# Last edge pass of a two-layer graph network kernel: projection in three passes, y one turn later, messages in PSUM, one-hot on ScalarE, another order of loads

## The reference

```python
# layer 0: attention over the edges of each receiver, 8 heads of 32
qkv = x @ W_qkv.T + b_qkv                      # Q, K, V
att = einsum('mhd,mhd->mh', Q[receivers], K[senders]) * INV_SQRT_DK
e = exp(att - seg_max[receivers]);  denom = segment_sum(e, receivers)[receivers]
out = segment_sum((e / denom)[:, :, None] * V[senders], receivers)
x = layernorm(x + out @ W_ff.T + b_ff)
# layer 1: messages from the senders' type embedding and the edge attributes
W = (edge_attr_64 @ W_dist + b_dist) * cut[:, None]
msgs = embed_table[node_type_100][senders] * W
agg = segment_sum(msgs, receivers)
x = layernorm(x + concatenate([x, agg], axis=1) @ W_comb + b_comb)
```

## Time and profile before

| | |
|---|---|
| median of 3 runs | 1124.53 us (1122.92 to 1125.94) |
| the profiled execution | 1127.21 us, span 1125.5 us |
| mean granted TensorE clock of the span | 0.978 |
| busy share: PE, DVE, ACT, POOL | 94%, 82%, 71%, 72% |
| span of the last edge pass | about 747 us to the end |

### The profile page before, as it was taken

The page is one execution under the profiler, slowest core; times in us unless marked ns, Lnnn a source line. Parts: engine busy times, 40 slices in busy tenths (PEclk is TensorE's granted clock), DMA queues, the critical chain, the costliest instruction groups (busy, mean ns, idle before and its releaser), DMA issues.

```text
span 1125.5 us, 25645 instructions
## 1 busy us (share of the span) xinstructions
PE 1058.2 (94%) x7302; PEld 983.2 (87%) x7302; DVE 918.4 (82%) x2643; ACT 802.3 (71%) x2452; POOL 811.4 (72%) x656
## 2 busy tenths in 40 slices
PE   5889999999999999999979799989999999999993
PEld 4679999999999999999858588879989888889882
DVE  5867888888888888888998889758888888888882
ACT  3876777777777777777767688875666666666663
POOL 5588878787888788886788888844666666666663
PEclk9999999999999999999989899989999999999997
DMA  4866666666666666665545457765666666666640
GB/s 152 305 241 215 229 228 229 224 231 221 228 217 230 208 232 216 231 219 207 190 166 200 158 206 238 276 195 164 177 174 186 188 183 186 186 189 193 186 140 33
DMA packets 121388, 227.26 MB, mean 202 GB/s; under 512 B 33588, under 2 KB 61487, under 8 KB 121185
## 3 DMA queue, kind: packets, MB, share of 16 engines
q1 hardware_dynamic: 104000, 189.54, 50.6%
q0 software_dynamic: 17248, 36.08, 11.3%
HBM read 137.84 MB, written 93.59 MB: 206 GB/s over the span
## 4 chain that ended last, share of the span: by engine, by line
PE 52%; DVE 26%; issue 10%; ACT 7%; SPq 2%; DVEq 1%; DMA 1%; POOL 0%; ACTq 0%; POOLq 0%
PE ps L852 7%; DVE num L1619 5%; PE ps L831 5%; PE ps L891 4%; PE ps L890 4%; PE ps L892 4%; PE ps L847 4%; PE ps L845 4%; PE ps L846 4%; DVE zeT L1630 3%; DVE est L1656 3%; DVE agg L1643 3%; PE ps L888 2%; ACT t L1196 2%; DVE msg L1639 2%
## 5 line engine op out<-in xcount | busy, mean ns | idle before, releaser
L682 POOL TENSOR_TENSOR zin<-xin,bff_row 128x1024 f32<-128x1024 f32 x98 | 233.1, 2379 | 39.3 <-DVE stat L1414 18.5
L1442 DVE SCALAR_TENSOR_TENSOR yn<-ps,r,bc 128x256 f32<-128x256 f32 x391 | 169.0, 473 | 64.0 <-PE ps L847 40.5
L852 PE MATMUL ps<-w_mix,zT 128*128 128x256 f32 x780 | 189.4, 394 | 10.1 <-ACT zT L1092 5.4
L852 PEld LDWEIGHTS ps<-w_mix,zT 128*128 128x128 f32 x780 | 147.8, 197 | 34.4 <-ACT zT L1092 10.7
L1107 ACT ACTIVATE junk<-yn 128x256 f32<-128x256 f32 x391 | 157.8, 415 | 12.3 <-DVE yn L1442 12.0
L743 POOL TENSOR_TENSOR ev<-abc,v 128x512 f32<-128x512 f32 x49 | 62.0, 1266 | 115.5 <-DVE zeT L1630 115.5
L1414 DVE BATCH_NORM_STATS2 stat<-zin 128x6 f32<-128x256 f32 x391 | 135.3, 407 | 1.9 <-issue 1.5
L724 POOL DMA_INDIRECT ty<-in_node_type_dram,src_i x98 | 103.2, 1053 | 25.7 <-issue 23.1
L730 POOL DMA_INDIRECT xd<-in_x_dram,idx x98 | 94.8, 967 | 36.1 <-PE ps L876 13.8
L755 POOL DMA_INDIRECT out_dram<-oe,idx x98 | 101.1, 1032 | 25.4 <-issue 20.2
L845 PE MATMUL ps<-mix_hi,z_hi 128*128 128x256 f32 x392 | 114.0, 291 | 2.8 <-DVE z_lo L1479 2.8
(11 more groups left out here) (212 smaller groups left out, 3377.0 us busy)
## 6 DMA issues: line engine op xcount, KB each, us to landing
xin<-in_x_dram SPq DMA_DIRECT2D x97, 512.0 KB, 4.4
out_dram<-on SPq DMA_DIRECT2D x97, 512.0 KB, 2.9
xd_o<-xdT SPq DMA_DIRECT2D x49, 256.0 KB
v_o<-vT SPq DMA_DIRECT2D x49, 256.0 KB, 2.0
v<-v_o SPq DMA_DIRECT2D x49, 256.0 KB
xd<-xd_o SPq DMA_DIRECT2D x49, 256.0 KB, 4.2
abc<-a_o SPq DMA_DIRECT2D x196, 64.0 KB
sbc<-same_o SPq DMA_DIRECT2D x49, 128.0 KB, 3.8
```

The source lines that it names most:

```text
L682: pool.tensor_tensor(z, xx, bb, ALU.add).then_inc(n_z, 1)
L852: last = mm(ps[0:np_, half(g, j), (j % 2) * D:(j % 2 + 1) * D], zT[:, g % 2, k, j * P:j * P + np_], w_mix[:, k, :], start=k == 0, stop=k = ...
L1442: last = dve.scalar_tensor_tensor(out=yn[0:np_, q, j * D:(j + 1) * D], in0=ps[0:np_, half(g, j), (j % 2) * D:(j % 2 + 1) * D], scalar=r1[0 ...
```

## The change

It edits the last edge pass alone, save for the weight's parts. (1) `ff` uses `wff_hi`, `wff_lo` and high and low parts of `num`, 12 fp32r matmuls in place of 4 fp32 ones; ScalarE makes the high part (`sum_high`), GpSimd the low part (`sum_low`), and VectorE once the low part of the weight. (2) VectorE's turn computes y of block i-3, not i-2, ahead of `edge_z`, so the second norm and the scatter come a turn later as well. (3) The product of `messages` is written back into PSUM bank 7, and the two scans read it there; `filters` now waits for the scans of the block before. (4) The one-hot is made by ScalarE in two instructions, `Square(type - lane)` and `Relu(1 - square)`; `lane` holds negative numbers for it. (5) In each turn SP issues `same_load` first, then values and attention, attributes, receivers, types.

```diff
@@ memories @@
-    wff = sb("wff", [P, DC, D])
+    wff_hi, wff_lo = (sb(n, [P, DC, D], F32R) for n in ("wff_hi", "wff_lo"))
...
+    num_hi, num_lo = (z_lo[:, 1, c, :].rearrange("p (c n) -> p c n", c=2) for c in range(DC))
@@ sync @@
         for i in range(-1, B):
-            if 2 <= i + 3 < B:
-                type_load(i + 3)
-                attribute_load(i + 3)
+            if 2 <= i + 1 < B:
+                same_load(i + 1)
             if 2 <= i + 2 < B:
                 value_load(i + 2)
                 attention_load(i + 2)
-            if 2 <= i + 1 < B:
-                same_load(i + 1)
+            if 2 <= i + 3 < B:
+                attribute_load(i + 3)
             if 2 <= i < B:
                 receiver_load(i)
+            if 2 <= i + 3 < B:
+                type_load(i + 3)
@@ gpsimd @@
+        def sum_low(n):
+            pool.wait_ge(e_num, 2 * (n + 1))
+            pool.wait_ge(e_nh, n + 1)
+            after(pool, e_ffp, n)
+            pool.tensor_tensor(flat(num_lo), flat(num[:, n % 2]), flat(num_hi), ALU.subtract).then_inc(e_nl, 1)
...
-        for i in range(-1, B + 4):
+        for i in range(-1, B + 5):
...
-            if within(i - 4):
-                scatter(i - 4)
+            if within(i - 5):
+                scatter(i - 5)
+            if within(i):
+                sum_low(i)
             if within(i + 1):
                 weigh(i + 1)
@@ tensor @@
         def ff(n):
             par = n % 2
-            pe.wait_ge(e_num, 2 * (n + 1))
+            pe.wait_ge(e_nh, n + 1)
+            pe.wait_ge(e_nl, n + 1)
             after(pe, e_z, 2 * (n - 1))
             for c in range(2):
+                to = bank(FF[par])[:, c, :]
                 for k in range(DC):
-                    last = mm(bank(FF[par])[:, c, :], wff[:, k, c * P:(c + 1) * P], num[:, par, k, :], start=k == 0, stop=k == DC - 1)
+                    hi, lo = (w[:, k, c * P:(c + 1) * P] for w in (wff_hi, wff_lo))
+                    mm(to, hi, num_hi[:, k, :], start=k == 0, stop=False)
+                    mm(to, hi, num_lo[:, k, :], start=False, stop=False)
+                    last = mm(to, lo, num_hi[:, k, :], start=False, stop=k == DC - 1)
...
         def filters(n):
             pe.wait_ge(e_atT, n + 1)
-            after(pe, e_msg, n)
+            after(pe, e_agg, 2 * n)
@@ scalar @@
+        def onehot(n):
+            par = n % 2
+            act.wait_ge(e_tb[par], 16 * (n // 2 + 1))
+            act.activation(off[0:SPECIES, :], tybc[0:SPECIES, par, :], ACT.Square, bias=lane[0:SPECIES, 0:1]).then_inc(e_off, 1)
+            act.wait_ge(e_off, n + 1)
+            after(act, e_embp, n)
+            act.activation(hot[0:SPECIES, :], off[0:SPECIES, :], ACT.Relu, bias=one_col[0:SPECIES, :], scale=-1.0).then_inc(e_hot, 1)
...
+        def sum_high(n):
+            act.wait_ge(e_num, 2 * (n + 1))
+            after(act, e_ffp, n)
+            act.activation(flat(num_hi), flat(num[:, n % 2]), ACT.Copy).then_inc(e_nh, 1)
...
+            if within(i):
+                sum_high(i)
+            if within(i - 4):
+                edge_final(i - 4)
             if within(i - 3):
-                edge_final(i - 3)
+                edge_squares(i - 3)
...
             if within(i + 1):
                 embedding_copy(i + 1)
-            if within(i - 2):
-                edge_squares(i - 2)
+            if within(i + 2):
+                onehot(i + 2)
@@ vector @@
+            dve.tensor_tensor(wff_lo[:, k, :], ps[:, A + 1, D:2 * D], wff_hi[:, k, :], ALU.subtract).then_inc(s_wlo, 1)
...
-            after(dve, e_agg, 2 * n)
-            dve.tensor_tensor(msg[:], bank(7), emb[:], ALU.mult).then_inc(e_msg, 1)
+            dve.tensor_tensor(bank(7), bank(7), emb[:], ALU.mult).then_inc(e_msg, 1)
...
-                dve.tensor_tensor_scan(out=agg[:, now, c, :], data0=sbc[:, par, :], data1=msg[:, c, :],
+                dve.tensor_tensor_scan(out=agg[:, now, c, :], data0=sbc[:, par, :], data1=bank(7)[:, c, :],
...
-        for i in range(-2, B + 3):
+        for i in range(B + 4):
             if within(i):
                 sums(i)
                 messages(i)
+            if within(i - 4):
+                edge_rstd2(i - 4)
             if within(i - 3):
-                edge_rstd2(i - 3)
+                edge_y(i - 3)
             if within(i - 1):
                 edge_z(i - 1)
-            if within(i + 2):
-                onehot(i + 2)
             if within(i - 2):
                 edge_stats(i - 2)
-                edge_y(i - 2)
```

More of the change, by code:

```diff
@@ L218, in build @@
     hot = lp("hot", [P, EB], F32R)
-    emb, msg = (lp(n, [P, 2, EB]) for n in ("emb", "msg"))
+    off = lp("off", [P, EB])
+    emb = lp("emb", [P, 2, EB])
     ev, num, zeT = (lp(n, [P, 2, 2, EB]) for n in ("ev", "num", "zeT"))
@@ L358, in build @@
     e_hot = sem("onehot_ready")
+    e_off = sem("squared_type_distances")
     e_embp = sem("embedding_product")
@@ L366, in build @@
     e_zp = sem("edge_z_transposed")
+    e_nh = sem("attention_sum_high_parts")
+    e_nl = sem("attention_sum_low_parts")
     e_zh = sem("edge_z_high_parts")
@@ L865, in weight_transposes @@
             after(pe, s_wtc, 3 * k)
-            after(pe, s_wlo, 2 * k)
+            after(pe, s_wlo, 3 * k)
             for r in range(4 * DC):
@@ L1042, in _ @@
                 pe.wait_ge(s_wtc, 6)
-                pe.wait_ge(s_wlo, 4)
+                pe.wait_ge(s_wlo, 6)
                 pe.wait_ge(s_brow, 2)
@@ L1132, in weight_copies @@
             act.activation(w_hi[:, k, 2 * D:3 * D], ps[:, A + 1, 0:D], ACT.Copy).then_inc(s_wtc, 1)
-            act.activation(wff[:, k, :], ps[:, A + 1, D:2 * D], ACT.Copy).then_inc(s_wtc, 1)
+            act.activation(wff_hi[:, k, :], ps[:, A + 1, D:2 * D], ACT.Copy).then_inc(s_wtc, 1)
         def bias_copies():
@@ L1266, in _ @@
         scaled(0)
-        for i in range(-1, B + 3):
+        onehot(0)
+        for i in range(-1, B + 4):
             if within(i + 1):
@@ L1406, in edge_indices @@
             dve.wait_ge(s_lane, 1)
-            dve.tensor_copy(lane[:], lane_i[:]).then_inc(s_idx, 1)
+            dve.tensor_scalar(lane[:], lane_i[:], -1.0, None, ALU.mult).then_inc(s_idx, 1)
         def stats(g):
@@ L1616, in sums @@
             after(dve, e_num, 2 * n)
-            after(dve, e_ffp, n - 1)
+            after(dve, e_nh, n - 1)
+            after(dve, e_nl, n - 1)
             for c in range(2):
@@ L1642, in messages @@
             for c in range(2):
-                dve.tensor_tensor_scan(out=agg[:, now, c, :], data0=sbc[:, par, :], data1=msg[:, c, :],
+                dve.tensor_tensor_scan(out=agg[:, now, c, :], data0=sbc[:, par, :], data1=bank(7)[:, c, :],
                                        initial=agg[:, past, c, EB - 1:EB] if n else 0.0, op0=ALU.mult, op1=ALU.add).then_inc(e_agg, 1)
-        def onehot(n):
-            par = n % 2
-            dve.wait_ge(e_tb[par], 16 * (n // 2 + 1))
-            after(dve, e_embp, n)
-            dve.tensor_scalar(hot[0:SPECIES, :], tybc[0:SPECIES, par, :], lane[0:SPECIES, 0:1], None, ALU.is_equal).then_inc(e_hot, 1)
         def edge_stats(n):
```

## The result

| | before | after |
|---|---|---|
| median of 4 runs | 1124.68 us (1122.92 to 1125.94) | 1150.2 us (1149.77 to 1151.3) |
| ratio, 95% interval | | 1.0231 (1.0215 to 1.0247) |
| span of the profiled execution | 1125.5 us | 1148.1 us |
| scans of block 2 and of block 48 start | 760.49, 1093.65 us | 757.31, 1113.23 us |
| a turn, mean of these 46 | 7.243 us | 7.737 us |

The change makes the kernel 2.3% slower. The forecast was 1159 us, with a range of 1136 to 1174.

A forecast was written before the change was run, and what follows sets the result against it. VectorE's loop from z to z was to bound at 7.95 us a turn against 7.24: 46 turns give 32.5 us, with start and end +35, so 1162 us profiled, median 1159, range 1136 to 1174.

The forecast's parts named there:

- What bounded before: Last edge pass: the round trip VectorE, ScalarE, VectorE bounds at 7.24 us a turn, TensorE close behind at 7.10.
- y one turn later: VectorE's idle 0.36 and 0.48 us for ScalarE go; `ev` is late next, and the scans wait for it.
- The exclusion: Scans of `sums`, with two SBUF inputs, and a GpSimd product stop each other; the low parts' 1.27 us is added.
- it gets faster: Rival: products don't stop this pass's scans, TensorE bounds at 6.80 us, 1106 us; decides at 0.59 of 1.27; chance 0.15.
- The new loop: VectorE from z to z: 3.53 us until the scans, then 4.36, giving 7.89 us a turn, 7.95 with PSUM.
- The near tie: GpSimd before the scans: z's low parts ready about 2.1 us after z, weighing ends at 2.29; scans taken as second.
- Messages in PSUM: Aggregate's scans, with one SBUF input, are no longer stopped; PSUM scans and product together cost 0.06 us a turn.
- Start and end: Outside the steady turns: 1.5 us for a later start, 1 us for one more turn at the end.
- Marks first: SP's queue: the load of the same-receiver marks goes ahead of six others; a 2.50 us wait before turn 2's scan goes.
- Projection and one-hot: TensorE's product falls from 1.72 to 1.42 us; VectorE loses 0.34; ScalarE comes to at most 6.5 and doesn't bound.
- GpSimd's turn bounds: Rival: both scans go ahead of z's low parts and GpSimd's loop takes 7.70 us a turn, 1147 us; chance 0.16.
- The edit of TensorE shows nothing: Projection's saving of 0.30 us falls on TensorE, which then waits over 1 us a turn; included in the forecast.

The follow-up runs named there:

- only_y: The kernel before with y of block i-3 ahead of `edge_z`, second norm and scatter a turn later, nothing else of the change: 1148.59 us, ratio 1.0198.
- marks_psum: The changed kernel with the marks of `sums` read from PSUM, written there by one more matmul a turn: 1131.19 us, ratio 1.0045.
- scatter_sooner: scatter_last with the scatter of block i-4 in place of i-5: 1114.41 us, ratio 0.990.
- weigh_first: The changed kernel with GpSimd's `weigh` ahead of `sum_low` and without its wait for `edge_z`: 1124.64 us, ratio 0.9988.
- y_back: The changed kernel without part 2 on any engine, y of block i-2 behind the statistics again: 1122.45 us, ratio 0.9973.
- scatter_last: The changed kernel with GpSimd's order `weigh`, `sum_low`, scatter, `edge_z_low`, and without `weigh`'s wait for `edge_z`: 1115.63 us, ratio 0.9921.

## Why the prediction held, point by point

**What bounded before** and **y one turn later**: shown. The idle 0.36 and 0.48 went, `ev` became late next, and only_y has the same loop without the rest.

**The exclusion** is shown by marks_psum, above all by block 2, where the product stands as in the change and the scans aren't held. The rival *it gets faster* falls with it: a turn loses 1.02 us (2.32 against 1.30) where 0.59 would have decided. What that rival took for the floor, TensorE's row (6.80 in its sum, 6.87 measured), is reached in another way, once the products miss the scans: 1114 us in scatter_sooner, where it had 1106. The Trainium skill's page "SBUF — State Buffer" (section "SBUF: two separate sides") has it that the first to start holds the ports for one whole instruction; the trace agrees scan by scan in the change (2.39 and 1.62 us) and in weigh_first (1.59), and the pair of 4.11 us in scatter_sooner is not explained by it.

**The new loop** is the step that was mis-sized: 7.95 us forecast, 7.75 measured, over 46 turns the 9 us between 1159 and 1150. Of the 0.20, 0.11 lies from z to the scans' end: 3.53 + 1.30 = 4.83 were put there, 4.72 are measured. The prediction took it that low parts that come inside the first scan make the same sum. It isn't quite the same: of their 1.27 us only 1.02 is felt. Part of the product lies beside the scans at both ends. It takes 1.62 us where it takes 1.28 alone, so if it waited first it ran from 912.12 to 913.40; the first scan's own record ends 912.30, and the second scan ends 913.95, 0.55 after the product, where its record is 0.72 when nothing holds it. y_back agrees: of an overlap of 0.57 us, 0.36 is felt. That the product waited first is inferred from its length. The near tie that it worked out, 2.1 against 2.29 us after z, was the wrong way round: the high parts were ready only 2.49 us after z (ScalarE waited for mix), and the low parts started 2.62 us after z, with the scans already running since 2.40.

**Messages in PSUM** were taken at 0.06, and are another part of it: 1.38 us for the scans and 0.67 for the product against 1.40 and 0.67, so 0 to the trace's resolution. The last 0.03 of the 0.20 are the aggregate's scans with the reciprocals, 1.54 against 1.57. The estimate by the Trainium skill's page "VectorE: DVE Perf Modes" (section on the TRN2 errata), 0.13 us a turn, is not what this trace shows; the measurement decides. That the aggregate's scans are free of the exclusion is shown by scatter_last; in the change itself no product of GpSimd lies beside them (the low part of the sums starts 908.32, when they are over), so there it brings nothing.

**Start and end** were +1.5 and +1, and are +0.7 and +3.0. The turn more at the end is bare to a larger part than the scatters alone: VectorE waits there again for ScalarE's root, 0.90 and 1.95 us in the last turns.

**Marks first** was costed by the start alone. What the sum left out is that the one-hot's move makes the types' load wait for ScalarE, and that the new order of loads is what keeps this from the scans: nothing in the change's time, 27 us without it. The prediction asked what the moved load overtakes, and not which engine each load waits for.

**Projection and one-hot** came as costed: 1.51 us of passes where 1.42 were put (1.72 before), and ScalarE's load, 39.26 of 50 us of a 7.74 us turn, is 6.1 us where 6.5 was the bound. Neither bounds.

*GpSimd's turn bounds* gave 1147, nearer to 1150 than the forecast, but by a mechanism that isn't there: GpSimd waits 0.57 us for z and 0.31 for ScalarE in the turn shown above, and with the same work runs turns of 6.87. *The edit of TensorE shows nothing* held: TensorE waits 0.68 us for y before mix.

## What to carry to other kernels

Before an instruction is moved out of a wait, write down what ran on the other engines during that wait: here 0.84 us of idle VectorE were the cover of GpSimd's products, and removing them cost 1.6 us (1.02 of exclusion, 0.59 for `ev`). On engines that exclude each other, order the rows so that their instructions with two SBUF inputs don't meet; dropping one wait and reordering GpSimd's row made 1150 us into 1114. And when an operation changes its engine, look at each load that waits for it: at the head of a queue it holds all that stand behind.

## What was not expected of the hardware

- Between a pair of scans GpSimd gets in, and who is held depends on the start: a product that came 0.22 us after the scans began, in the first, held the second (2.39 us for the pair, itself 1.62); one that came at 0.90, in the second, was itself held (1.59) and the pair took 1.40.
- Two products without a gap between them held a pair for both, 4.11 us, though the first of them began 1.04 us after the pair did; by the pattern above it should have waited itself. The same happened in all four turns of scatter_last and scatter_sooner in which VectorE came 0.31 us late. The scatter right ahead of the product doesn't explain it: in block 48 of scatter_last, where VectorE wasn't late, a product that followed a scatter in the same way, 0.93 us after the scans began, did wait (1.55), and the scans weren't held. Why it didn't wait in the four is open.
- A small exclusion can make turns alternate: 6.87 and 7.56, 7.14 and 7.59, 7.00 and 7.36 us. The mean of a group of instructions hides this; the starts in order of time show it.
- One more matmul of 256 columns, with a single row to contract, made TensorE's turn 0.45 us longer (7.32 against the 6.87 of weigh_first). 0.33 us of idle time stand ahead of its weight load, so not all of it is the matmul itself.
